# A graph layer's edge gathers: the first 32, not 24, read raw rows, and the padded last gather is left out

## What is computed

```
xn  = layernorm(x)                                     # per row
W_r = sum over b of comp[r, b] * basis[b]              # 8 relations from 4 bases
agg[d] += xn[s] @ W_type        for each edge (s, d, type)
g   = layernorm(gelu(agg + xn @ loop_w + h_bias + xn)) * gamma + beta
mix = query @ batchnorm(softmax(key over nodes)^T @ value)     # query, key, value from xn
x1  = x + g + mix
out = x1 + relu(relu(xn1 @ W1[e] + b1[e]) @ W2[e] + b2[e])     # xn1 = layernorm(x1), e = argmax of router logits
```

## Time and profile before

| what | before |
|---|---|
| median of three runs | 633.35 us (632.36 to 633.79) |
| span of the profiled execution (first to last instruction) | 629.7 us |
| the profiled execution's own time | not recorded apart from its span; the median is 3.65 us above the span |
| mean granted TensorE clock, as a share of 2.4 GHz | 0.949 |
| PE busy | 535.7 us (85%) |
| POOL busy | 430.2 us (68%) |
| DVE busy | 375.0 us (60%) |
| ACT busy | 200.2 us (32%) |
| chain of work that ended last | PE 60%, POOL 11%, DMA 9%, DVE 9%, issue 6% |

### The profile page before, as it was taken

How to read it: one execution, slowest core, us unless ns; L and a number is a source line. 1 busy time by engine, 2 the same in 40 slices (tenths; PEclk the granted TensorE clock), 3 DMA queues, 4 the chain that set the end, 5 groups by cost and what they waited for, 6 DMA issues and landing times.

```text
span 629.7 us, 10658 instructions
## 1 busy us (share of the span) xinstructions
PE 535.7 (85%) x3193; PEld 435.8 (69%) x3193; DVE 375.0 (60%) x1392; ACT 200.2 (32%) x402; POOL 430.2 (68%) x449
## 2 busy tenths in 40 slices
PE   0667998989899877899999999999999983389990
PEld 0556997877677765687887878787877851278880
DVE  6879777443343344555666666666666666626882
ACT  5673402100033001114343343424243331155430
POOL 7747777777777777777777777777777720474662
PEclk9979999999999988899999999999999986589996
DMA  8973333333333354335454545444444428473221
GB/s 278 273 224 109 107 105 102 104 101 101 109 101 106 105 158 136 107 102 154 131 150 135 151 130 155 144 143 149 136 151 134 147 86 243 120 214 112 84 86 40
DMA packets 41410, 85.38 MB, mean 136 GB/s; under 512 B 10809, under 2 KB 23034, under 8 KB 41155
## 3 DMA queue, kind: packets, MB, share of 16 engines
q0 software_dynamic: 21968, 61.03, 33.4%
q1 hardware_dynamic: 18372, 22.95, 11.6%
q10 hardware_dynamic: 1008, 0.65, 0.3%
HBM read 71.79 MB, written 12.81 MB: 134 GB/s over the span
## 4 chain that ended last, share of the span: by engine, by line
PE 60%; POOL 11%; DMA 9%; DVE 9%; issue 6%; ACT 1%; DVEq 0%; POOLq 0%; ACTq 0%
PE ps L929 23%; PE ps L991 13%; PE ps L980 6%; DMA gath<-xn_d,src_i 6%; POOL gath L591 5%; POOL acc_raw L591 4%; PE ps L1198 3%; PE ps L1207 3%; PE ps L946 3%; POOL both L637 2%; PE ps L957 2%; DVE raw_stats L1315 1%; DMA rel_of<-in_relation_of 1%; DMA both<-rows_d,inv_i 1%; PE ps L1014 1%
## 5 line engine op out<-in xcount | busy, mean ns | idle before, releaser
L591 POOL DMA_INDIRECT gath<-xn_d,src_i x264 | 254.5, 964 | 80.4 <-issue 68.2
L929 PE MATMUL ps<-wmat,gath 128*128 128x80 f32 (+1 forms) x1056 | 154.7, 287 | 15.8 <-DMA gath<-xn_d,src_i 14.6
L929 PEld LDWEIGHTS ps<-wmat,gath 128*128 128x128 f32 x1056 | 139.6, 194 | 33.6 <-DMA gath<-xn_d,src_i 18.4
L1385 DVE TENSOR_TENSOR wmat<-hit,wts 128x576 f32<-128x576 f32 (+1 forms) x100 | 63.1, 631 | 135.5 <-PE ps L929 135.4
L591 POOL DMA_INDIRECT acc_raw<-xn_d,src_i x104 | 100.9, 970 | 39.1 <-issue 25.9
L1410 DVE TENSOR_TENSOR acc_raw<-acc_raw,ps 128x144 f32 (+1 forms) x392 | 88.6, 267 | 43.0 <-PE ps L929 41.8
L929 PE MATMUL ps<-wmat,acc_raw 128*128 128x144 f32 x512 | 76.0, 292 | 11.9 <-ACT acc_raw L699 5.7
L929 PEld LDWEIGHTS ps<-wmat,acc_raw 128*128 128x128 f32 x512 | 68.2, 190 | 20.7 <-issue 11.4
L991 PE MATMUL ps<-wk_et,acc_raw 128*128 128x256 f32 (+1 forms) x200 | 53.5, 392 | 0.1
L991 PE MATMUL ps<-wq_wv,acc_raw 128*128 128x256 f32 (+1 forms) x200 | 52.1, 384 | 0.0
L637 POOL DMA_INDIRECT both<-rows_d,inv_i x25 | 24.2, 967 | 40.2 <-DVE inv_i L1685 32.8
(11 more groups left out here) (232 smaller groups left out, 719.4 us busy)
## 6 DMA issues: line engine op xcount, KB each, us to landing
rows_d<-both SPq DMA_DIRECT2D x24, 256.0 KB, 2.6
gath<-xn_d,src_i POOLq DMA_INDIRECT x264, 2.8
both<-in_x SPq DMA_DIRECT2D x24, 128.0 KB
both<-in_x SPq DMA_DIRECT2D x4, 640.0 KB, 9.8
xn_d<-both SPq DMA_DIRECT2D x4, 640.0 KB
acc_raw<-in_w_t SPq DMA_DIRECT2D x1, 2080.0 KB
acc_raw<-in_w_t SPq DMA_DIRECT2D x1, 2048.0 KB, 7.2
acc_raw<-xn_d,src_i POOLq DMA_INDIRECT x104, 2.8
```

Source lines behind the costliest of these rows:

```text
L591: g.indirect_dma_start(place_of(n), None, table, bass.IndirectOffsetOnAxis(ap=src_i[:, n:n + 1], axis=0)).then_inc(done, 16)
L929: ins = t_.matmul(ps_edge[quarter][:, m * w:(m + 1) * w], place_of(n)[:, m * P:(m + 1) * P], wmat_tiles[:, k, 0:w], start=k == pair[0], st ...
L1385: d.tensor_tensor(made, hit[:, :, 0:width(q)].unsqueeze(2).to_broadcast([P, w, B, width(q)]), wts[:, :, cut].rearrange("p b t -> p t b").u ...
```

## The change

`RAW` goes from 3 to 4: 32 blocks are gathered from raw `x` and normalised where they land. The 32 raw blocks fill the ring of 32 slots once, in the slots that they had before. The clears of the accumulator tiles that stood beside octet 2 move beside octet 3. In octet 48 seven blocks are gathered and multiplied, not eight.

```diff
--- before.py
+++ after.py
@@ -37,6 +37,7 @@
 ROWG = 4
 WROW = ROWG // PAIR
 NWIN = ETAB // PAIR
+USED = -(-E // P)
 TG = P // R
 TC = ETAB // TG
 CB = 512 // (TG * B)
@@ -56,7 +57,7 @@
 HIGH = 16
 STAGE = KD * B * 4
 EARLY = 16
-RAW = 3
+RAW = 4
 FIRST_CLEAR = 6
 NEAR, MIDDLE = HIGH - 2, EARLY + 2
 EPS = 1e-5
@@ -607,7 +608,7 @@
                 if q == EARLY:
                     pool.wait_ge(rel_ready, 1)
                 if q >= RAW:
-                    for k in range(OCT):
+                    for k in range(min(OCT, USED - OCT * q)):
                         gather(OCT * q + k)
 
             edge_schedule(octet)
@@ -724,7 +725,8 @@
                     raw_root(q + 1)
                     raw_normalise(q + 1)
                 if q + 1 >= RAW and q + 4 < HIGH:
-                    clear_tile(q + 4)
+                    for t in range(FIRST_CLEAR if q + 1 == RAW else q + 4, q + 5):
+                        clear_tile(t)
                 if beside == "chain":
                     if q - 1 in STEP:
                         gelu(STEP[q - 1], once)
@@ -913,7 +915,7 @@
             def edges(q, quarter):
                 if quarter % 2 == 0:
                     pe.wait_ge(wmat_built, 2 * q + quarter // 2 + 1)
-                pair = range(PAIR * quarter, PAIR * quarter + PAIR)
+                pair = range(PAIR * quarter, min(PAIR * quarter + PAIR, USED - OCT * q))
 
                 pe.wait_ge(added, KD * (4 * q + quarter + 1))
                 for m in range(KD):
```

## The result

The change makes the kernel faster by about half of what was forecast. Four executions took 627.63 to 630.41 us, median 629.45; four of the kernel before on the same chip took 632.18 to 633.79, median 632.86. The ratio is 0.994, 95% interval 0.9922 to 0.9958: 3.4 us less between the medians, where 7.0 were forecast and 626.3 us was the predicted time.

A forecast was written before the change was run, and what follows sets the result against it. The prediction took the start of POOL's gather stream, with its 7.69 us hole, to bound the edge stage. Span 629.7 less 7.0 (7.39 less 0.4 for stores) is 622.7, plus 3.65 around it: 626.3 us, range 624.6 to 629.6.

The forecast's parts named there:

- The stream's start: POOL's gathers: eight more raw ones fill the 7.69 us hole, gather 32 starts earlier, gain 7.0 us (6.0 to 7.4).
- price of the stores: Before gather 32: table stores landing later beside the raw gathers, taken as 0.4 us, between 0 and 1.35 us.
- The rival of half their speed: Table stores run at half speed beside the gathers, gather 32 starts at 49.4, time 630.4 us; chance 0.08.
- a rule of the Trainium skill: At the table stores: engines alternate between queues packet by packet, halving the stores' speed; 630.4 in place of 626.3 us.
- Octet 3 on TensorE: PE's octet 3 starts at 72.2, 2.4 us later, covered by PE's waits for gathers.
- the moves: `judge` to octet 4 on DVE: 0, at most 2.4 us; ACT's clears, later beside octet 3: cost 0.
- the last gather: End of the edge stage: leaving out this gather and its products gains 0, at most 1.9 us, hidden by DVE.
- The chain's step: PE's chain: runs at PE's pace, with 10.12 us from step to step, unchanged.
- The step that failed: Gather stream up to the chain: the 7.69 us hole goes through to the end; first chain step 7 us earlier.
- PE's slack: PE between 42 us and the chain: 17.6 us of waits for gathers, of which 9.4 must be given up.
- the second rival: PE's waits are latency of single gathers, not stream pace, so no gain: 633.4 us; chance 0.05.
- The range: Whole kernel: 8 in 10 for 624.6 to 629.6 us, the upper end for a late store tail.

The follow-up runs named there:

- the kernel with the product cut in four: Changed kernel with VectorE's edge-weights instruction of 128x576 cut into four of 128x144; 623.59 us (ratio 0.9854).
- the raw octet alone: Kernel before with 32 raw gathers instead of 24, the last gather and its products kept; 628.51 us (ratio 0.9948).
- the one-input twin: Changed kernel with an added VectorE reduction of one 128x576 SBUF tensor ahead of each edge-weights product; 635.74 us (ratio 1.0029).
- TensorE kept at work: Changed kernel with two repeated edge products more per quarter in octets 20 to 23; 627.42 us (ratio 0.9908).
- the run that was to stretch the lock: Changed kernel, edge-weights product uncut, with one repeated edge product more per half octet in octets 8 to 15; 628.80 us (ratio 0.9944).
- the two kernels with TensorE longer in octets 8 to 15: Changed kernel with one repeated edge product more per half octet there: edge-weights product uncut, 628.80 us, or cut in four, 630.65 us.
- the twofold one: Changed kernel with VectorE's edge-weights product cut into two pieces of 128x288; 624.06 us (ratio 0.9846).
- both kernels with the product cut in four: VectorE's edge-weights product cut into four of 128x144, in the changed kernel (623.59 us) and in the kernel before (630.10 us).

## Why the prediction was half right

*The stream's start*: right. No hole, gather 32 at 45.36 (forecast 44.95 to 46.3), no price of the stores. The rival of half their speed (gather 32 at 49.4) did not come about, nor did the time that the prediction worked out by a rule of the Trainium skill, that each engine takes turns between its queues (page "DMA: Bandwidth & Descriptors", section "Queues, rings and completion order"). No run shows the turns themselves.

*Octet 3 on TensorE, the moves, the last gather*: right in place, but for the clock. Octet 3 at 72.08, with a first pair of 2.26 us at half clock that no term of the sum held, and the last gather within 1.3 us of nothing by itself.

*The chain's step*: right, and so is that it is PE's pace.

```profile
453.01 1.92 PE L982 MATMUL ps<-cmat,both 128*128 128x512 f32 x4
...
463.13 1.92 PE L982 MATMUL ps<-cmat,both 128*128 128x512 f32 x4
```

It is 10.12 us as before, and from 400 to 460 us PE has no wait in either trace. The gathers come to the same step by a hold of about 0.11 us (eight of 1.25 us and that hold). In the kernel with the product cut in four one step of POOL takes 9.99 us (429.49 to 439.48), and the step of PE in that stretch is 10.12 all the same (436.51 to 446.63).

*The step that failed* is that the hole "goes through to the end", with a gather and its gap at 1.25 us, "a little more where a gather is longer", and so a chain that starts 7 us earlier. The first chain product starts 1.23 us earlier, before and then after:

```profile
263.70 1.98 PE L980 MATMUL ps<-cmat,both 128*128 128x512 f32 x4 [0.61 <-DVE bias L1615]
```

```profile
262.47 1.99 PE L982 MATMUL ps<-cmat,both 128*128 128x512 f32 x4 [0.59 <-DVE bias L1617]
```

With the raw octet alone, where POOL has no wait in octet 24, it starts at 258.07, and with the product cut in four as well at 254.59. The pace of the stream is not fixed. While TensorE has a backlog its half octet is 4.10 us; three gathers are 3.75; and the weights' product, which follows TensorE, holds one gather in three until the 0.35 us between them is used up. The earlier stream and the later octet 3 keep the backlog for about four octets more, so this lasts longer, and about 3 us of the 7 go there. That the holds cost time, and that a second input in SBUF makes most of them, is shown by the runs. That the 4.10 us lock the two is read from the spacing in four traces (after, the raw octet alone, the one-input twin, TensorE kept at work); the run that was to stretch the lock did not show its price, so this part is argued.

*PE's slack*: too coarse. I summed waits over 212 us and let PE give them up anywhere. In octets 21 to 24 the small products wait for one another whatever the gathers do, TensorE's clock falls there, by how much differs between traces (222 to 262 us: 0.87 before, 0.79 after, 0.96 with the raw octet alone), and the ring of eight hands this to POOL. The warning stood in the second rival: one wait was longer than the gap between two gathers.

*The range*: 629.45 lies 0.15 us inside the upper end of 624.6 to 629.6. That end was set for a late store tail, which did not come, and neither of the two losses was in the sum. That the time lies inside is luck.

Of the profiled pair's 6.98 us, then, 3.1 went to holds up to octet 16 and 2.35 in octet 24; 0.7 came back in between, where the execution of before was held too, and 0.45 behind. The last 1.6 us of the span difference lie behind the edge stage. From gather 384 to the end the traces differ by more than that, though the program behind octet 48 is the same: 129.9 us in before, 131.6 in after, 129.8 with the raw octet alone, 135.2 and 135.7 in the two kernels with TensorE longer in octets 8 to 15. What sets it is open, so a few us between two single traces are not by themselves the stream's.

The fourfold cut with 32 raw gathers is the fastest measured, 623.59 us, 9 us under the kernel before; the twofold one is as fast within their intervals. Either together with TensorE kept at work was not tried.

## What to carry to other kernels

A stream of issues with no gap in its waits can still be slowed by how long each issue takes: read the spread of its durations, and what another engine runs at its start, before a lead is carried to the end of the program. Where two engines run freely at nearly commensurate paces, look for long instances at equal distances, as the 4.10 us here: a small interference can keep the two in step, and a lead that is won early is spent on it. Where latency-bound work drops TensorE's clock, products that nobody needs may be worth a try; here they came with a likely gain of some 2 us.

## What the runs showed that was not expected

- Where a VectorE product of two inputs in SBUF already runs by itself, a gather is held for what is left of it at the gather's start, less 0.12 to 0.13 us. If a weights' product starts 0 to 0.2 us after the gather, the gather takes its usual 0.945 us (12 gathers of after, 0.942 to 0.947). The additions into the accumulator, with one input in PSUM, start 0.1 or 0.2 us ahead of a gather 81 times in after and hold none (0.942 to 0.949).
- Two tensor inputs are not the only case. The `tensor_scalar` of `finish_row`, with one tensor of 128x256 in SBUF and two per-partition scalars, held single gathers for 0.04 us (raw octet alone), 0.11 us (both kernels with the product cut in four) and 0.14 us (that cut with TensorE longer). Where it started less than 0.15 us ahead of a gather, the gather took its 0.945 us, and the `tensor_scalar` mostly 0.46 us in place of 0.41.
- Pieces that follow closely can hold together: eight pieces of 0.23 us, 0.14 apart, held a gather for up to 0.53 us, four of 0.30 us, 0.22 apart, for at most 0.16. Why they differ is not shown.
- A VectorE instruction on 36 columns with two per-partition scalars takes 0.315 us, as long as a product of 144 columns (0.30).
